# GpSimd splits each image's theta rows at step nine after the image's last step, in place of step five (two-layer convolution and attention kernel, one core)

## What is computed

```python
# layer 0: 8 groups of 8 channels; all products of two and of three channels of a group
p2 = x[:, :, I2] * x[:, :, J2]
y2 = einsum('bgihw,goi->bgohw', p2, W2) + b2
p3 = x[:, :, I3] * x[:, :, J3] * x[:, :, K3]
y3 = einsum('bgihw,goi->bgohw', p3, W3) + b3
l = x + y2 * beta2 + y3 * beta3 * 0.1
# layer 1
g = clip(bn1(conv1x1(l, w_inside)), 0, 6)
theta = l[:, :32]
f = softmax(einsum('niab,nicd->nabcd', theta, theta), over ab)
f = softmax(f, over cd)
out = einsum('nabcd,nicd->niab', f, g)
out = bn2(depthwise3x3(out)) + l
```

## Time and profile before

| | us |
|---|---|
| median of 3 runs | 5319.7 (5316.72 to 5321.96) |
| the profiled execution, its own time | 5314.02 |
| its span, first to last instruction | 5312.2 |
| layer 0, to the last selection that was late | 794.03 |
| mean granted TensorE clock | 0.996 |

### The profile page before, as it was taken

How to read it: one execution, slowest core, us unless ns; L and a number is a source line. 1 busy time by engine, 2 the same in 40 slices (tenths; PEclk the granted TensorE clock), 3 DMA queues, 4 the chain that set the end, 5 groups by cost and what they waited for, 6 DMA issues and landing times.

```text
span 5312.2 us, 88127 instructions
## 1 busy us (share of the span) xinstructions
PE 5210.2 (98%) x32182; PEld 2524.8 (48%) x32182; DVE 4411.7 (83%) x8859; ACT 5093.6 (96%) x2948; POOL 4423.8 (83%) x1854
## 2 busy tenths in 40 slices
PE   8988999999999999999999999999999999999999
PEld 3333335454545454444545454544454545444454
DVE  7877788888888888888888888888888888888887
ACT  7777789999999999999999999999999999999998
POOL 6656655688888998898899888899888899889988
PEclk9999999999999999999999999999999999999999
DMA  7787762222223222222322222222222322222222
GB/s 145 150 161 151 154 128 51 56 62 62 62 62 62 62 62 55 55 51 54 62 62 55 62 61 56 57 56 62 62 62 62 62 62 62 61 56 52 52 41 48
DMA packets 227275, 380.45 MB, mean 72 GB/s; under 512 B 158181, under 2 KB 175262, under 8 KB 216734
## 3 DMA queue, kind: packets, MB, share of 16 engines
q1 hardware_dynamic: 225728, 373.82, 34.2%
q10 hardware_dynamic: 1118, 1.00, 0.1%
HBM read 259.08 MB, written 102.74 MB: 68 GB/s over the span
## 4 chain that ended last, share of the span: by engine, by line
PE 67%; ACT 15%; issue 8%; DVE 3%; POOL 3%; SPq 3%; DMA 1%; DVEq 0%; ACTq 0%; POOLq 0%
PE at_AV L1284 32%; PE at_S L1243 18%; ACT at_ring L1027 11%; PE at_AV L1290 9%; ACT at_ring L1033 4%; PE l_TY L607 3%; SPq L459 3%; PE at_AV L1280 2%; PE l_SEL L596 2%; DMA l_TH<-l_YO 1%; DVE at_ring L1100 1%; PE l_TY L614 1%; DVE l_U L564 1%; POOL l_LO L500 1%; POOL l_XX L491 1%
## 5 line engine op out<-in xcount | busy, mean ns | idle before, releaser
L1100 DVE TENSOR_SCALAR_CACHE_REDUCE at_ring<-at_S 128x1344 f32<-128x1344 f32 (+2 forms) x2352 | 2882.4, 1242 | 457.6 <-PE at_S L1243 438.8
L977 POOL TENSOR_TENSOR at_ZP<-at_ZP,at_ring 128x1568 f32<-128x1568 f32 x640 | 2263.3, 3571 | 146.0 <-ACT at_ring L1033 136.0
L1284 PE MATMUL at_AV<-at_ring,at_GT 128*64 128x392 f32 x12800 | 2299.8, 500 | 6.8 <-issue 5.9
L1027 ACT ACTIVATE at_ring<-at_ring,at_NM 128x3136 f32<-128x3136 f32 x784 | 2275.6, 2903 | 12.5 <-DVE at_NM L1109 11.4
L1033 ACT ACTIVATE at_ring<-at_ring,at_RZ 128x3136 f32<-128x3136 f32 x784 | 2276.9, 2904 | 0.0
L1284 PEld LDWEIGHTS at_AV<-at_ring,at_GT 128*64 128x64 f32 x12800 | 854.5, 137 | 1146.3 <-issue 1108.9
L1243 PE MATMUL at_S<-at_THM,at_THS 128*128 128x448 f32 x5376 | 1381.0, 386 | 11.5 <-DVE at_ring L1100 9.1
L1243 PEld LDWEIGHTS at_S<-at_THM,at_THS 128*128 128x128 f32 x5376 | 926.5, 188 | 631.6 <-DVE at_ring L1100 290.7
L998 POOL TENSOR_TENSOR at_OUTB<-at_OUTB,at_ZB 128x1568 f32<-128x1568 f32 x246 | 877.6, 3567 | 16.8
L1290 PE MATMUL at_AV<-at_ring,at_ones 128*32 128x392 f32 x7168 | 676.9, 498 | 2.9 <-DVE at_ACC L1193 2.9
L564 DVE TENSOR_TENSOR l_U<-l_TY,l_XB 128x512 f32<-128x512 f32 x784 | 487.5, 683 | 164.7 <-PE l_TY L607 164.4
(11 more groups left out here) (86 smaller groups left out, 2713.3 us busy)
## 6 DMA issues: line engine op xcount, KB each, us to landing
at_THM<-hld SPq DMA_DIRECT2D x128, 392.0 KB, 6.3
at_THS<-hld SPq DMA_DIRECT2D x256, 192.0 KB, 4.0
l_X<-in_x SPq DMA_DIRECT2D x124, 392.0 KB, 7.1
at_CIN<-att SPq DMA_DIRECT2D x62, 406.0 KB, 7.7
at_ZB<-rzd SPq DMA_DIRECT2D x62, 406.0 KB, 7.7
yd<-l_YO SPq DMA_DIRECT2D x128, 196.0 KB, 5.1
att<-at_ACC SPq DMA_DIRECT2D x248, 98.0 KB
at_OUTB<-yd SPq DMA_DIRECT2D x62, 392.0 KB, 8.5
```

The lines of the kernel that those rows point to most:

```text
L977: e.tensor_tensor(z, z, v, ALU.add).then_inc(g_add, 1)
L1027: e.activation(v, v, ACT.Exp, bias=NM[:, i:i + 1], accum_out=ZS[:, i:i + 1]).then_inc(a_p1, 1)
L1100: e.tensor_scalar(ring[:, s % RING, SC * a_:SC * b].rearrange("p (b w) -> p b w", w=SC), PS[:, k % 2, bank:bank + b - a_, 0:SC], 1.0, None ...
L1284: ins = e.matmul(dst[64 * j:64 * j + 64, 0:QC], GT[fl.n % 2][:, keys_of(fl.n, t), :], ring[:, slot, q:q + QC], start=(i == 0), stop=(i == ...
```

## The change

The constant SPLIT_LATE goes from 5 to 9. GpSimd then runs split(n) behind parts(L + 9) and not behind parts(L + 5). Every other instruction, on every engine and queue, keeps its place. As an image has 6.125 steps, split(n) now stands behind the steps of image n+1 and some steps of image n+2. Images 30 and 31 (L = 189 and 195) are both split after the last step; before, image 30 was split behind parts(194), with parts(195) after it.

```diff
@@ -20,7 +20,7 @@
 CH = 512
 NX = 3
 EARLY = 8
-SPLIT_LATE = 5
+SPLIT_LATE = 9
 FOLD_AT = 24
 FIRST = (slice(0, CH), slice(CH, 3 * CH), slice(3 * CH, HW))
```

## The result

The changed kernel takes 5231.3 us (median, 5230.4 to 5232.0), the kernel before on the same chip 5318.2 us: 86.9 us less, ratio 0.9836, 95% interval 0.9818 to 0.9853. Forecast were 5241 us, 79.1 us less. The profiled execution took 5232.02 us, its span is 5230.2 us.

What follows compares the result with a forecast made beforehand. TensorE was taken to bound the kernel, stopped in layer 0 by GpSimd's late XX. Waits of 66.0 plus clock 13.1, costs 0, made 79.1 us off the 5319.7 median: 5240.6, about 5241 us, range 5231 to 5263.

Steps and rivals of the forecast that it cites:

- Mechanism and place: Layer 0: GpSimd's wait for TH keeps it from its full lead, so TensorE waits for XX; splitting four steps later cures it.
- the signs listed ahead: Layer 0: few late selections, TH wait under 60 us, selection wait well over 100, clock 1.00, layer 1 some 79 us earlier.
- First term, the waits: TensorE in layer 0: all 31 waits for GpSimd's XX go, 66.0 us gained.
- Second term, the clock: TensorE in layer 0: slow-clock stretches behind late selections go with the waits, 13.1 us gained, bounds 0 and 13.1.
- The step that failed: Whole kernel: median stands 5.7 us above the profiled execution, so 79.1 is taken from 5319.7, giving 5240.6 us.
- The queue it is moved past: SP's queue: the wait for split(n-1) ahead of TH(n) has about 8 us to spare; cost zero.
- SP's own time: SP in layer 0: fullest image issues 21.7 us, just inside 22.2; cost taken as 0, upper bound 18 us.
- The DMAs: DMA queues in layer 0: share 88%, near 163 GB/s; TH landing up to 6.4 us against a cover of 12; cost 0.
- Slow stretches that stay without waits: Layer 0 clock, rival 1: waits go but slow stretches, or a few waits, stay; 5253.7 us, chance 9%.
- SP or DMAs as the bound: Layer 0, rival 2: SP or DMAs stretch an image to 23.4 us, giving 37 us back; 5278 us, chance 8%.
- No lead: GpSimd in layer 0, rival 3: it cannot build a lead, so nothing changes; 5320 us, chance 3%.
- Slower by the wait for the split before: SP in layer 0, rival 4: waiting for split(n-1) delays TH(n), 71 us more; 5391 us, chance 2%.

Runs made afterwards that it cites:

- seven: SPLIT_LATE = 7, only the constant changed, against the kernel before: 5232.2 us, ratio 0.9838.
- twelve: SPLIT_LATE = 12, only the constant changed, against the kernel before: 5232.2 us, ratio 0.9840.
- five casts more: The changed kernel with five more casts of TH into HO in each split: 5232.8 us, ratio 0.9838 to the kernel before.
- the new order at six: SPLIT_LATE = 6, with SP issuing the load three images ahead behind the TH and yd copies: 5232.8 us, ratio 0.9843 to the kernel before.
- six: SPLIT_LATE = 6, only the constant changed, SP's order as before, against the kernel before: 5246.1 us, ratio 0.9865.
- the first profile: The kernel before, unchanged, the profiled execution that the prediction was read from: 5314.0 us.
- the second profile of the kernel before: The kernel before, unchanged, profiled again: 5322.0 us.
- the third: The kernel before, unchanged, profiled a third time: 5313.7 us.
- the last profiles: The kernel before, unchanged, third profile, 5313.7 us, and the changed kernel, unchanged, second profile, 5233.6 us.
- fifteen: SPLIT_LATE = 15, only the constant changed, against the kernel before: 5419.1 us, ratio 1.0188.

## Where the prediction held, and the step that failed

**Mechanism and place: right.** The wait for TH had used up GpSimd's lead; four steps later the copy has landed and the lead covers the split. Shown from both sides: steps seven and twelve give the same time, more than twice the work gives the same time, and the signs listed ahead all came: late selections none, GpSimd's wait for TH 29.3 us (under 60), its wait for selections 193.7 (well over 100), SP's wait for closings 4.3 us an image (about 4), the first score 81.3 us earlier (79), layer 1 as long as before. "GpSimd gains 1.57 us of lead a step" is borne out too: it fills its buffers in every image.

**First term, the waits: right but for 2 us.** 66.0 us went, all of it; three profiles of the kernel before give 66.0, 66.8 and 67.2. To each belong the 0.07 us that the list misses. I had them in the step, 3.62 where the free step is 3.611, and so left 183 x 0.011 = 2 us out of the gain.

**Second term, the clock: right for the execution it was read from, too small for slower ones.** "No wait, no fall: I take all 13.1" held in the six profiles that have no late selection of over 0.3 us (step nine twice, seven, twelve, five casts more, and the new order at six): no ten-us stretch of layer 0 below 1.00. Where waits remained, at six, five of them, the clock was 0.83 in 300 to 310, and lower again behind the wait at 348.88. For the profiled execution the size is right as well: 15.3 less the 2 is 13. The rule that I took from the Trainium skill (TensorE: Matmul & The Clock Gate, Part 1), full clock for activity, slow for idleness, agrees in kind. Which wait brings a fall stays open: in the first profile eight of 31 did, one of 2.37 us among them and one of 3.44 not, and in the second the clock was 0.83 in 220 to 230, at a wait of 1.83.

**The step that failed** is the one from the profiled execution to the median, and with it the size of the clock term: "The median of the runs stands 5.7 above that execution, so I forecast 5319.7 - 79.1." I carried this offset over as if it were fixed and would be there after the change, and took the 13.1 us of one quick execution for the clock term of the median one. What the runs showed: the second profile of the kernel before, 8 us longer than the first, has 22 us of slow clock, and the third, as quick as the first, 10. The mean granted clock of the other executions of the kernel before, where it is on record, points the same way: 0.994 to 0.995 in all from 5319.8 us up, 0.995 to 0.997 below. After the change the median lies 0.7 below its profiled execution. The account closes: 79.1, and 2.9 between the two profiled executions (2 from the step, 0.7 in layer 1, the rest in rounding and the start), and 4.2 + 0.7 from the medians, make 86.9. That the 4.2 are all clock, which would make the term some 17 in place of 13.1, is an estimate from these profiles, as no median execution was profiled. The offset also differs from chip to chip: on the chip of the last profiles the median of the kernel before was 5314.3 and the one execution of the changed kernel 5233.6, 80.7 less, close to the 79.1.

**The costs taken as zero: right, but one with less room than its reason said.** *The queue it is moved past:* SP never waited at L455; room for three more steps, as twelve shows. *SP's own time:* in image 16 it was used up to the end. The load behind it is followed by TH of image 17 without a gap:

```profile
415.90 1.81 SPq L422 DMA_DIRECT2D l_X<-in_x  x4
417.81 4.95 SPq L459 DMA_DIRECT2D l_TH<-l_YO  x8
```

SP waited for 31 of 32 closings; this was the one it did not wait for. The cover took it. *The DMAs:* a share of 0.86 and 169 GB/s from 100 to 700 us, for 0.88 and 163 forecast. I looked at the copy's longest landing (6.4) and at the mean share, and not at what stands ahead of it in the queue. The bound of 6.4 did not hold, one DMA of the copy now took 9.1 us; the cover of 12 did. At step six that omission cost 13 us (first score at 732.12 for 719.38). The Trainium skill's rise of the time of an HBM access under high load (DMA: Bandwidth & Descriptors, Latency and other measured facts) does not show in the stores to HBM: their median landings from 100 to 700 us were 5.4 (yd), 3.4 (HO) and 1.9 us (LO) before and are 5.8, 3.3 and 1.9 now, so no run here shows 2 us more.

**The rivals.** Slow stretches that stay without waits: not seen. SP or DMAs as the bound: no, though SP had one image without a gap. No lead: no. Slower by the wait for the split before: real, but at fifteen, not at nine.

## What to carry to other kernels

When an in-order engine feeds the bound engine and also has to wait for something from behind it, ask first whether it is idle while it waits; if so, move the waiting work later until the round trip and the work together fit the buffers, and look for both edges, the second being the buffer that the late work holds. An engine that runs through at full clock pays its waits more than once: take the slow stretches behind them as part of the same gain, and size them over several executions. An offset between the profiled execution and the median may itself be what a change removes.

## What the runs showed that I had not expected

The kernel before spread over 5311.6 to 5324.0 us in some thirty executions, the changed one over 5230.4 to 5233.6 in five, and all versions without late selections of over 0.3 us over 5230.4 to 5235.9 in 21: taking the waits away took most of the spread as well. And eight small copies that stood 3 us behind a load of 1.6 MB and first loads of layer 1 landed 5.3 us after their last issue, against 1.6 in most images; a change in the order of one queue, with not a byte less, brought the kernel at step six from a ratio of 0.9865 to 0.9843 and took 11.5 us out of layer 0. No version tried beats step nine by more than a measurement can tell.
